# Later places for the third and fourth score products of a unit among the transposes and v products of the unit before it

## What is computed

```python
# x: (2, 1024, 512); 32 query heads and 8 key heads of 128; feed-forward width 1792
xn = _layernorm(x)
q = xn @ Wq.T                      # 32 heads, rotary
k = rotary part xn @ Wkr.T, rest (xn @ Wdk.T) @ Wupk.T     # 8 heads
v = (xn @ Wdk.T) @ Wupv.T          # 8 heads
scores = jnp.einsum('bhqd,bhkd->bhqk', q, k) * scale
scores = jnp.where(causal, scores, -1e9)
out = jnp.einsum('bhqk,bhkd->bhqd', jax.nn.softmax(scores), v) @ Wo.T
ffn = (silu(xn @ W_gate.T) * (xn @ W_up.T)) @ W_down.T
return x + out + ffn
```

## Time and profile before

| | us |
|---|---|
| median of 3 runs (lowest to highest) | 2465.45 (2463.36 to 2466.46) |
| the profiled execution | 2469.72 |
| its span, first to last instruction | 2467.5 |
| PE busy, share of the span | 2366.8 (96%) |
| DVE, ACT, POOL busy | 1483.8 (60%), 1134.6 (46%), 939.7 (38%) |

### The profile page before, as it was taken

One profiled execution on the slowest core, in us unless ns is written; L12 is line 12 of the kernel. 1 busy time (PEld: TensorE's weight loads), 2 busy tenths in 40 slices (PEclk: granted clock), 3 DMA queues, 4 the chain that ended last, 5 costly groups with the idle time before them and its releaser, 6 DMA issues.

```text
span 2467.5 us, 38965 instructions
## 1 busy us (share of the span) xinstructions
PE 2366.8 (96%) x11840; PEld 1975.6 (80%) x11840; DVE 1483.8 (60%) x3641; ACT 1134.6 (46%) x2217; POOL 939.7 (38%) x813
## 2 busy tenths in 40 slices
PE   6999999989899999999999999999999999999998
PEld 5777877768688888878887888788888878888886
DVE  4343334424576666766676767666666666676765
ACT  2442624335354544444454545354545444454544
POOL 1000000000454444545454545455444545454543
PEclk9999999999999999999999999999999999999999
DMA  5676757788312121231313152312222121213110
GB/s 191 188 285 184 257 168 247 266 274 286 131 49 98 44 96 63 83 104 36 104 43 104 35 192 84 119 44 95 67 81 95 43 104 44 103 35 112 35 52 18
DMA packets 103736, 287.26 MB, mean 116 GB/s; under 512 B 9056, under 2 KB 42336, under 8 KB 92512
## 3 DMA queue, kind: packets, MB, share of 16 engines
q1 hardware_dynamic: 101408, 280.53, 33.9%
q10 hardware_dynamic: 2112, 4.19, 0.4%
HBM read 200.80 MB, written 83.89 MB: 115 GB/s over the span
## 4 chain that ended last, share of the span: by engine, by line
PE 63%; issue 7%; DVE 3%; ACT 3%; DMA 2%; POOL 2%; SPq 1%; ACTq 0%; DVEq 0%; POOLq 0%
PE qb L1113 14%; PE ob L1153 14%; PE ob L1168 13%; PE scores L1131 12%; PE ptb L1142 9%; DMA ff_raw<-in_ffw 2%; DVE pT L1065 1%; ACT pT L1018 1%; PE ring L874 1%; POOL prob L979 1%; SPq L601 1%; ACT prob L1005 1%; SPq L608 0%; POOL late_qT L989 0%; POOL q_cos L985 0%
## 5 line engine op out<-in xcount | busy, mean ns | idle before, releaser
L979 POOL TENSOR_TENSOR prob<-prob,rinv 128x896 f32<-128x896 f32 (+7 forms) x512 | 583.2, 1149 | 407.4 <-DVE rinv L1083 405.8
L1018 ACT ACTIVATE pT<-ptb 128x512 fp32r<-128x512 f32 x576 | 335.9, 594 | 568.7 <-PE ptb L1142 561.9
L1005 ACT ACTIVATE prob<-prob,nmax 128x896 f32<-128x896 f32 (+7 forms) x512 | 396.2, 774 | 329.5 <-DVE nmax L1044 324.2
L1153 PE MATMUL ob<-pT,v_sb 128*128 128x512 f32 x1728 | 509.4, 413 | 13.6 <-DVE pT L1065 11.1
L1065 DVE TENSOR_TENSOR pT<-ptb,pT 128x512 fp32r<-128x512 f32 x576 | 390.9, 688 | 126.6 <-ACT pT L1018 119.8
L1044 DVE CUSTOM_DVE_ANT_0 prob<-scores,mask 128x896 f32<-128x896 f32 (+7 forms) x512 | 384.6, 753 | 44.6 <-issue 30.5
L985 POOL TENSOR_TENSOR q_cos<-q_cos,q_sin 128x512 f32<-128x512 f32 x125 | 161.8, 1294 | 563.9 <-DVE q_cos L1061 563.9
L1113 PE MATMUL qb<-xT,wq 128*128 128x512 f32 x1500 | 362.6, 391 | 5.2 <-DVE q_cos L1061 3.6
L1153 PEld LDWEIGHTS ob<-pT,v_sb 128*128 128x128 f32 x1728 | 297.9, 190 | 83.8 <-DVE pT L1065 42.4
L1142 PE MATMUL ptb<-ident,prob 128*128 128x128 f32 x2304 | 341.9, 275 | 7.2 <-POOL prob L979 6.5
L1131 PE MATMUL scores<-kT,late_qT 128*128 128x448 f32 (+3 forms) x1536 | 339.5, 356 | 1.4
(11 more groups left out here) (86 smaller groups left out, 2254.0 us busy)
## 6 DMA issues: line engine op xcount, KB each, us to landing
wq<-w_parts SPq DMA_DIRECT2D x126, 512.0 KB, 3.8
w_parts<-stage SPq DMA_DIRECT2D x32, 1024.0 KB, 4.9
ff_raw<-in_ffw SPq DMA_DIRECT2D x56, 384.0 KB, 3.8
k_parts<-stage SPq DMA_DIRECT2D x128, 128.0 KB, 2.4
v_parts<-stage SPq DMA_DIRECT2D x64, 256.0 KB, 3.6
w_raw<-in_wqo SPq DMA_DIRECT2D x32, 512.0 KB, 6.0
kT<-k_parts SPq DMA_DIRECT2D x16, 1024.0 KB, 7.1
v_sb<-v_parts SPq DMA_DIRECT2D x16, 1024.0 KB, 9.0
```

The costliest lines, as they stand in the source:

```text
L979: nc.gpsimd.tensor_tensor(prob[:, n % 2, h, 0:W], prob[:, n % 2, h, 0:W], rinv[:, hd % 8:hd % 8 + 1].broadcast_to([P, W]), ALU.mult)\
L1005: nc.scalar.activation(prob[:, n % 2, j, 0:W], prob[:, n % 2, j, 0:W], ACT.Exp, bias=nmax[:, hd % 8:hd % 8 + 1], scale=-1.0, accum_out=rsu ...
L1018: nc.scalar.activation(pT[:, t % 3, HI], ptb[t % 2][:], ACT.Copy).then_inc(pT_hi, 1)
L1153: mm = nc.tensor.matmul(ob[:], v_sb[e % 2][:, x, j], pT[:, t % 3, y], start=(j == 0 and (x, y) == (HI, HI)), stop=(is_last(kind, n, j) and ...
```

## The change

The table of places is changed in two numbers.

```diff
-PLACES = (("S", 0, 0.0), ("W", 0, 0.15), ("S", 1, 0.2), ("S", 2, 0.3), ("S", 3, 0.7), ("Q", 0, 1.0))
+PLACES = (("S", 0, 0.0), ("W", 0, 0.15), ("S", 1, 0.2), ("S", 2, 0.5), ("S", 3, 0.75), ("Q", 0, 1.0))
```

## The result

The changed kernel took 2473.22 us (median of 8 runs, 2468.80 to 2481.53), the kernel before 2464.37 in 8 runs on the same chip (2462.06 to 2466.89). The ratio is 1.0038 with a 95% interval of 1.0023 to 1.0052: slower, by 8.85 us between the medians. Forecast were 2473.1 us, and a loss of 7.6.

What follows compares the result with a forecast made beforehand. TensorE, 63% of the chain, bounds the kernel, its v products waiting 42.4 us for VectorE's low halves. Terms 8.6 + 5.6 - 4.5 - 2.1 = +7.6 us on the 2465.45 median give 2473.1, range 2463 to 2480.

Steps and rivals of the forecast that it cites:

- No price for the move itself: TensorE in the heads: reordering the same products adds no pure work, same sum within 0.1 us; only waiting changes.
- Kind 5: 16 steps, 768 keys, predecessor of 5 blocks: last v product waits behind the fourth score product's maximum; +8.6 us.
- step 53: The step of kind 5 walked through, from its first score product to the next unit's; predicted to grow by 0.54 us.
- Kind 6: 16 steps, 896 keys, predecessor of 6 blocks: last low half waits behind the fourth score product's maximum; +0.35 each, +5.6 us.
- step 54: The step of kind 6 walked through, from its first score product to the next unit's; predicted to grow by 0.35 us.
- Kind 3: 16 steps, 128 keys, predecessor of 2 blocks: second transpose starts one small product earlier; gain 0.28 each, -4.5 us.
- Kind 2: 16 steps, 256 keys, predecessor of 3 blocks: last transpose goes ahead of the third score product; gain 0.1 to 0.13, -2.1 us.
- Kinds 7, 0, 1, 4: The other four kinds of step: the last transpose and the end keep their times; zero, within 0.05 us.
- The cover works: Rival: in kind 6 the moved fourth score product covers the last transpose's conversion, kind 5 loses nothing; -12.2 us, 2453.3; chance 0.10.
- Half as large: Rival: losses in kinds 5 and 6 are only 0.25 and 0.15 a step; -0.2 us, 2465.3; chance 0.20.
- Larger losses: Rival: first transposes also wait 0.5 us for later normalising in kinds 5 and 6; 16 us more, 2489; chance 0.04.

Runs made afterwards that it cites:

- dve_swap: Changed kernel with VectorE's list alone altered: the last transpose's low half goes ahead of the fourth score product's maximum in kinds 5 and 6; 2456.74 us, ratio 0.9956.
- act_swap5: Changed kernel with ScalarE's list alone altered: in kind 5 the last transpose's copy goes ahead of the third exponential; one run, 2469.46 us.
- s2_only: Changed kernel with the fourth score product back at 0.7, leaving only the third's move to 0.5; 2470.62 us, ratio 1.0023 to the kernel before.
- s3_only: Kernel before with only the fourth score product's place moved, 0.7 to 0.75; 2462.45 us, ratio 0.9979.
- best_b: Kernel before with score product places set separately for predecessors of 2, 3, 6, 7 and 8 blocks, old places elsewhere; 2450.31 us, ratio 0.9941.
- best_c: best_b with one number altered: third score product at 0.5 instead of 0.3 behind 7 blocks; 2441.86 us, ratio 0.9906 to the kernel before.

## Why the prediction was right

**No price for the move itself.** It holds. In dve_swap both kinds are within 0.02 and 0.07 us of the sums without a wait, 15.37 and 17.06, with S2 and S3 at their new places.

**Kind 5.** The working said P4 would start 12.39 into step 53 (1380.78, from an S0 at 1368.39); it started at 12.41 (1381.35 - 1368.94). Each stage of the walk came as written: S2's maximum, the exponential ahead of the copy, S3's maximum, the low half behind it. The step grew by 0.60 instead of 0.54: P4 was 0.44 late, the q product 0.11 more (0.81 behind P4 instead of 0.70, as said), and from the q product to the next S0 it took 2.75 us instead of 2.71, which the working had left out. So in this step the v product that waits costs 0.15 beside its wait. The term was +8.6 us. The 15 steps up to 117 grew by 8.7, 0.58 each, which gives +9.3 for 16. The sum of 7.7 over all 16 is lower because of step 125, which the execution of before ran at the lower clock; that the term seems too large by this sum is an accident of the pair. One stage of the walk was true but idle: the exponential ahead of T4's copy. act_swap5 shows that the term is S3's maximum alone.

**Kind 6.** Predicted +0.35, +5.6 us; measured +0.42, 6.6 in sum. The mechanism is as said, S3's maximum ahead of T5's low half. The words "in VectorE's new order" are not quite right: that order was the old one too, and the whole change is that S3 comes later. The q product started 15.09 into step 54 (1400.00 - 1384.91) where the walk had 15.04, and the next S0 lost 0.02 more.

**Kind 3.** Predicted -0.28, -4.5 us; measured -0.36, -5.5. T1 moved forward by 0.33, the 0.30 of the working plus 0.03. The upper bound of the term was the right value.

**Kind 2.** Predicted -0.10 to -0.13; measured -0.12 in the steady steps. What it is worth in the 8 steps at the loop's jump can't be read, since those vary by more from run to run.

**Kinds 7, 0, 1, 4.** Put at zero, within 0.05: +0.04, +0.02, -0.01 and nothing. In kind 0 that hides a cost of 0.32 of the third product's move, which the fourth's takes away, as s2_only shows. The 0.04 of kind 7 isn't explained: with the fourth or the third product moved alone it is 19.27 and 19.28.

**The sum.** +7.6 predicted, +8.4 for the steady steps of the first pair, +8.85 between the medians. At equal clocks in step 125 the steady steps come to about +10, or +9 if kind 2 gains its 0.12 at the loop's jump too, which can't be read. So the losses were some 2.3 us larger than predicted (kinds 5, 6 and 7), the gain of kind 3 1.0 larger, and the rest lies in what kind 2 is worth at the jump. That 2473.1 met 2473.22 to a tenth is luck: the forecast started from 2465.45, and the kernel before took 2464.37 in the comparison, 1.1 less, while the difference came out 1.25 larger. The interval of the difference alone reaches from 5.7 to 12.8 us.

**The rivals.** "The cover works" decided at the point that the text named, whether S3's maximum is out of the way of T5, and it wasn't. dve_swap and s3_only show that the gain it counted in kind 6 is real once that is mended. "Half as large" is excluded, since both steps grew by the full size and more. "Larger losses" is excluded by the waits for normalising, 6.7 us in 5 places against 6.5 in 5.

**Right for the median, not for the profiled run.** The forecast started from a profiled execution and carried the difference over to the median. For the profiled execution of the changed kernel it would have failed, 2475.1 said and 2467.0 found. The steps that the argument was about grew by 8.4 us, and other stretches hid as much in that execution. Why single runs of the changed kernel lay further apart (12.7 us) than those of the kernel before beside them (4.8) isn't settled. In the experiments the kernel before spread over 10.7 as well, and the changed one over 7.6 when it was run again, so it may be nothing. The clock has a part in the spread. Of the 17 runs of the kernel before beside the first experiments, the four at a mean granted clock of 0.990 took 2461.58 to 2465.58 us and the six at 0.986 or 0.987 took 2466.85 to 2472.27. The two profiled executions were at 0.988 (before) and 0.990 (changed).

## What to carry to other kernels

When independent work is moved on the busiest engine to cover a conversion, the move itself cost nothing here; look at what it puts ahead of the conversion in the lists of the engines that convert, since they don't pass over an instruction that isn't ready. Walk one step of each shape, transpose to copy to low half to use, and give each shape its own place if they differ: the same move of the third product cost 0.57 us in one kind and made a gain of 0.40 possible in another. And count the buffers: a transpose moved forward can come to wait for the bank of the one two before it.

## What the runs showed of the hardware

Away from the loop's jump the steps of the heads have the same medians to 0.03 us between executions, and between kernels where the order in them is the same, while whole executions of one kernel differ by 3 to 13 us. The difference sits elsewhere: ahead of the heads (604.7 to 614.1 us until they begin, over all profiled executions), at the hardware loop's jump back, where the pair of steps takes 25.6 us one time and 30.1 another, and in step 125. A change of 0.2% is read far better from the steps than from a span.

From step 3 to step 126 TensorE's lower clock level showed only at the loop's jump and in step 125, in no other step of any profiled execution. Six of the 11 profiled executions ran step 125 at a mean granted clock of 0.90, five at 1.00. Kernels with the same order of kind 5 differ by it: 15.10 us in best_b, 16.68 in best_a. In that step TensorE idles 2.25 us for a normalising in the kernel before, whose clock fell, and 2.26 in the changed kernel's first execution, whose clock didn't. What decides it isn't shown.

An earlier copy was worth nothing in act_swap5: it came 0.8 us sooner, and the wait it fed stayed 0.28. In kind 7 it was different: in best_b T6 waited for the bank that a late copy held, and with that copy ahead of the exponential, in best_c, the step was 0.61 us shorter. What comes last ahead of the waiting engine sets the time.
